# At the border to the second layer: four first row sums by VectorE, all x tiles turned before the products, source terms kept by ScalarE

## The reference, cut to what matters

```
# layer 1 (a graph attention; x is what the first layer left)
Wh = x @ W
e_src = Wh @ a[:d_out]
e_dst = Wh @ a[d_out:]
e = leaky_relu(e_src[:, None] + e_dst[None, :], 0.2)
mask = (adj > 0) | eye(N)
alpha = softmax(where(mask, e, -9e15), axis=1)
x = layernorm(x + alpha @ Wh)
# layers 2 and 3 (graph convolutions) use these sums of the same rows of adj:
rowsum = adj.sum(axis=1)
```

## Time and profile before

| | us |
|---|---|
| median of 3 runs | 3029.25 (3028.38 to 3029.67) |
| the profiled execution | 3032.35 |
| its span, from the first to the last instruction | 3030.6 |
| TensorE busy | 2951.2 (97%) |
| VectorE busy | 2098.9 (69%) |
| ScalarE busy | 1885.9 (62%) |
| GpSimd busy | 769.0 (25%) |

### The profile page before, as it was taken

How to read it: one execution, slowest core, us unless ns; L and a number is a source line. 1 busy time by engine, 2 the same in 40 slices (tenths; PEclk the granted TensorE clock), 3 DMA queues, 4 the chain that set the end, 5 groups by cost and what they waited for, 6 DMA issues and landing times.

```text
span 3030.6 us, 45417 instructions
## 1 busy us (share of the span) xinstructions
PE 2951.2 (97%) x16612; PEld 2181.2 (72%) x16612; DVE 2098.9 (69%) x3607; ACT 1885.9 (62%) x2705; POOL 769.0 (25%) x454
## 2 busy tenths in 40 slices
PE   8999999999999999999998899999999999999998
PEld 5777777777777777777776555555558888788886
DVE  6777777777777877787757977777535555565454
ACT  3677777777777777777775677777653333433332
POOL 2123321233212332133301455545501101000000
PEclk9999999999999999999999999999999999999999
DMA  6556676566755667566636333433179988989882
GB/s 186 158 170 198 198 211 180 170 197 196 216 162 180 199 188 227 156 184 205 189 101 257 124 125 130 148 126 125 32 183 214 214 200 201 221 209 217 199 200 58
DMA packets 412525, 534.42 MB, mean 176 GB/s; under 512 B 39440, under 2 KB 341776, under 8 KB 395920
## 3 DMA queue, kind: packets, MB, share of 16 engines
q1 hardware_dynamic: 387264, 445.00, 52.8%
q10 hardware_dynamic: 18144, 66.07, 7.1%
q0 software_dynamic: 6896, 20.45, 2.3%
HBM read 443.29 MB, written 88.08 MB: 175 GB/s over the span
## 4 chain that ended last, share of the span: by engine, by line
PE 80%; DVE 9%; issue 5%; DMA 3%; ACT 2%; POOL 1%; SPq 1%; DVEq 0%; POOLq 0%; ACTq 0%
PE at_o L609 12%; PE gl_four L1479 12%; PE at_turn L583 9%; PE at_turn L596 7%; PE gl_quad L1532 7%; PE gl_quad L1533 7%; PE gl_quad L1534 7%; PE at_score L583 4%; PE at_score L596 4%; PE gl_quad L1462 3%; DVE at_probs L869 2%; DVE at_bias L820 2%; PE gl_four L1505 2%; PE at_mixed L618 2%; DMA adjT<-at_probs 1%
## 5 line engine op out<-in xcount | busy, mean ns | idle before, releaser
L720 ACT ACTIVATE at_probs<-at_probs,at_minus_max 128x1024 f32<-128x1024 f32 x512 | 581.6, 1139 | 9.7 <-DVE at_minus_max L874 8.8
L869 DVE CUSTOM_DVE_ANT_0 at_probs<-at_turn,at_bias 128x1024 f32<-128x1024 f32 x336 | 407.3, 1212 | 170.2 <-PE at_turn L583 164.0
L506 POOL TENSOR_SCALAR at_masked<-at_bias 128x512 bf16<-128x512 f32 x180 | 378.2, 2116 | 537.7 <-DMA at_bias<-in_adj 405.4
L729 ACT ACTIVATE at_pT<-at_turn 128x1024 f32<-128x1024 f32 x342 | 346.0, 1024 | 235.4 <-PE at_turn L596 235.3
L609 PE MATMUL at_o<-at_pT,at_values 128*64 128x256 f32 x4096 | 470.3, 382 | 0.0
L1479 PE MATMUL gl_four<-gl_early,gl_first_wh 128*128 128x512 f32 x1024 | 462.3, 594 | 4.6 <-ACT gl_early L1604 4.6
L1629 ACT ACTIVATE gl_split<-gl_units 128x1024 fp32r<-128x1024 f32 x256 | 263.8, 1055 | 278.6 <-PE gl_quad L1534 278.6
L1532 PE MATMUL gl_quad<-gl_split,gl_rows_hi 128*128 128x512 f32 x1024 | 402.3, 393 | 5.0 <-DVE gl_split L1817 5.0
L609 PEld LDWEIGHTS at_o<-at_pT,at_values 128*64 128x64 f32 x4096 | 282.4, 137 | 172.8 <-issue 43.2
L583 PE MATMUL at_turn<-at_kT,at_q 128*128 128x512 f32 x1344 | 396.0, 416 | 10.3 <-DVE at_maxima L869 10.3
L1533 PE MATMUL gl_quad<-gl_split,gl_rows_hi 128*128 128x512 f32 x1024 | 398.5, 389 | 0.0
(11 more groups left out here) (135 smaller groups left out, 3871.0 us busy)
## 6 DMA issues: line engine op xcount, KB each, us to landing
gl_units<-adjT SPq DMA_DIRECT2D x512, 256.0 KB, 7.8
at_bias<-in_adj SPq DMA_DIRECT2D x128, 512.0 KB, 6.5
at_probs<-in_adj SPq DMA_DIRECT2D x256, 256.0 KB, 3.7
adjT<-at_probs SPq DMA_DIRECT2D x1024, 64.0 KB, 3.0
gl_first_weights<-in_adj SPq DMA_DIRECT2D x32, 2048.0 KB, 8.2
at_values<-v_heads ACTq DMA_DIRECT2D x126, 512.0 KB, 4.4
gl_early<-x SPq DMA_DIRECT2D x160, 128.0 KB, 2.6
x<-gl_early POOLq DMA_DIRECT2D x64, 128.0 KB, 2.8
```

Of the source, the lines that this page charges most:

```text
L506: pool.tensor_scalar(masked[:, g % MASKS, :], part, 0.0, MASKED / SCALE, ALU.is_equal, ALU.mult)\
L720: act.activation(part, part, ACT.Exp, bias=minus_max[:, k, t:t + 1], scale=1.0, accum_out=sums[:, k, t, pp:pp + 1]).then_inc(prob_ready, 1)
L729: act.activation(pT[:, j % PT_SLOTS, :], place[:], ACT.Copy).then_inc(pT_ready, 1)
L869: dve.tensor_tensor_reduce(out=ring[:, place_in_ring(u, pp), t, :], in0=place[:], in1=bias[:, t, at], scale=SCALE, scalar=LOWEST, op0=ALU. ...
```

## The change

Eight things change.

1. VectorE adds and masks only items 0 to 3 in the attention's last beats (`DVE_ROWS = 4`, two beats and not six).
2. ScalarE adds items 4 to 19: one behind each kept x unit 0 to 6 (`ROWS_BY_X`), the others behind kept Wh units (`ROWS_BY_WH`).
3. By the same rule as before, GpSimd now masks the odd items above 4 but 15: items 5, 7, 9 and 11 come to it beside 13. VectorE masks 4, 6, 8 and 10 later.
4. `v_xT` has 8 places, one for each unit, and takes the last two quarters of the second chunk's `weights`.
5. TensorE first turns x and makes the target terms for units 0 to 6 in a row, then makes Wh of units 0 and 1, turns the last unit, and makes the other Wh.
6. ScalarE keeps the source terms, in halves of two right behind each half of Wh (`keep_src`, scale -1); the next `make_wh` waits half by half.
7. Maxima, masks and logits on VectorE are put in a new order.
8. On SyncE, x tiles 16 to 29 come before adj quarter 2, x tiles 30 and 31 before the third quarter of the second chunk; that quarter waits for the Wh of four units and the fourth for all eight.

```diff
-    XT_RING = 4
-    DVE_ROWS = 12
+    DVE_ROWS = 4
-        v_xT = view(weights, HALF_BIG + 3 * CT * QC, XT_RING, DH * CN)
+        v_xT = view(weights, HALF_BIG + 2 * CT * QC, CHUNKS, DH * CN)
-        EARLY_ROWS = {0: (12, 13), 1: (14, 15), 2: (16,), 3: (17,), 4: (18,), 5: (19,)}
-        ROWS_IN_BEAT = {24: (0, 1), 25: (2, 3), 26: (4, 5), 27: (6, 7), 28: (8, 9), 29: (10, 11)}
+        ROWS_IN_BEAT = {24: (0, 1), 25: (2, 3)}
+        ROWS_BY_X = {u: (4 + u,) for u in range(CHUNKS - 1)}
+        ROWS_BY_WH = {0: (11, 12), 1: (13,), 2: (14, 15), 3: (16,), 4: (17,), 7: (18, 19)}
+        LAST_MASKS = (12, 14, 15)
+        WH_BEFORE_LAST = 2
...
-            if at == 23:
-                load_first_adj(sync, 2)
             if at == 25:
                 sync.wait_ge(shared.turned, shared.turned_but_one)
                 load_x(sync, 16, 30, 1)
+                load_first_adj(sync, 2)
                 load_first_adj(sync, 3)
...
-            sync.wait_ge(shared.turned, shared.beats)
+            load_x(sync, 30, 32, 2)
+            sync.wait_ge(wh_made, NT // 2)
             load_adj(1, 2)
-            load_x(sync, 30, 32, 2)
             sync.wait_ge(wh_made, NT)
             load_adj(1, 3)
...
             def make_wh(u):
-                wait(pe, wh_read, u)
...
                 for t in range(CT):
+                    if t % 2 == 0:
+                        wait(pe, wh_read, 2 * u - 1 + t // 2)
...
-            turn_x(pe, 1)
-            make_dst(0)
-            turn_x(pe, 2)
-            make_dst(1)
-            make_dst(2)
+            for u in range(CHUNKS - 1):
+                if u + 1 < CHUNKS - 1:
+                    turn_x(pe, u + 1)
+                make_dst(u)
             for u in range(CHUNKS):
-                if u + 3 < CHUNKS:
-                    turn_x(pe, u + 3)
+                if u == WH_BEFORE_LAST:
+                    turn_x(pe, CHUNKS - 1)
+                    make_dst(CHUNKS - 1)
                 if u == CHUNKS - 2:
                     turn_w()
                 make_wh(u)
-                if u + 3 < CHUNKS:
-                    make_dst(u + 3)
...
+            def keep_src(u, part):
+                m = CT * u + 2 * part
+                act.activation(minus_src[:, m:m + 2], quad[:, 2 * part:2 * part + 2, D:D + 1].rearrange("p a b -> p (a b)"),
+                               ACT.Copy, scale=-1.0).then_inc(wh_read, 1)
...
-                if c == 0:
-                    dve.wait_ge(wh_read, 1)
+                dve.wait_ge(wh_read, 2 * (c + 1))
...
-            def keep_src(u):
-                dve.wait_ge(wh_kept, 2 * (u + 1))
-                dve.tensor_scalar(minus_src[:, CT * u:CT * (u + 1)], quad[:, :, D:D + 1].rearrange("p a b -> p (a b)"),
-                                  -1.0, None, ALU.mult).then_inc(wh_read, 1)
...
+            masks(10)
+            for e in (10, 11):
+                read_max(e)
+            for e in LAST_MASKS:
+                masks(e)
+            for half in range(2):
+                if half == 1:
+                    keep_dst(CHUNKS - 1)
+                for e in LAST_MAXIMA:
+                    read_half_max(e, half)
+            make_shift(0)
+            for e in range(6):
+                logits(e)
+            keep_w()
+            for e in (16, 18):
+                masks(e)
+            for e in range(6, 10):
+                logits(e)
```

More of the change, by code:

```diff
@@ L1410, in make_dst @@
                 for half in range(DH):
-                    last = pe.matmul(upper[2 + u % 2], wa_wide[:, half, :], v_xT[:, u % XT_RING, half * CN:(half + 1) * CN],
+                    last = pe.matmul(upper[2 + u % 2], wa_wide[:, half, :], v_xT[:, u, half * CN:(half + 1) * CN],
                                      start=half == 0, stop=half == DH - 1)
@@ L1456, in turn_pair @@
                 if g < 2:
-                    pe.wait_ge(wh_read, CHUNKS)
+                    pe.wait_ge(wh_read, 2 * CHUNKS)
                 wait(pe, pT_ready, g - 1)
@@ L1632, in keep_xT @@
                 act.wait_ge(v_turned, u + 1)
-                wait(act, wh_made, CT * (u - XT_RING + 1))
-                act.activation(v_xT[:, u % XT_RING, :], four[:, 0:DH, :].rearrange("p a b -> p (a b)"), ACT.Copy)\
+                act.activation(v_xT[:, u, :], four[:, 0:DH, :].rearrange("p a b -> p (a b)"), ACT.Copy)\
                    .then_inc(v_ready, 1)
```

51 lines of the change are left out of this document (20 added, 31 removed).

## The result

| | before | after |
|---|---|---|
| median of 4 runs, us | 3029.46 (3028.38 to 3033.88) | 3012.37 (3006.57 to 3013.94) |
| profiled execution, us | 3032.35 | 3011.64 |
| its span, us | 3030.6 | 3009.5 |

The ratio is 0.9937, with a 95% interval of 0.992 to 0.9955: 14 to 24 us faster, where differences from 6 us on can be told from none. When the changed kernel was run again, its median was 3010.81 and the ratio 0.9936 (0.9923 to 0.9948). The forecast was 3010, the range 3004 to 3018.

A forecast was written before the change was run, and what follows sets the result against it. TensorE, busy 97% of the span, was taken as the bound, losing time idle or at half clock. First L1479 at 1669.3 against 1688.49 gives 19.2 us: 3032.35 - 19.2 = 3013.1 profiled, 3010 median; range 3004 to 3018.

The forecast's parts named there:

- Row sums hold back L908: Attention's end on VectorE: unneeded row sums delay the final L908; without them it comes at 1614.2, not 1626.15, 12 us sooner.
- The row of seven units: TensorE's turns and target terms for units 0 to 6: 2.59 us per unit, no long waits, ending at 1631.7.
- The small W just in time: Weight load the first products need: lands at 1631.6, as the row of turned units ends at 1631.7.
- x tiles 30 and 31: Input of the last turn: issued in the deferred 2 MB quarter's place, landing at 1638.7 instead of 1643.7, just in time.
- rival of late tiles: x tiles 30 and 31 still land at 1643.7: 4 us less gain, 15, or 3014; chance 0.10.
- The bubble: TensorE before the last target terms: 2.1 us idle, as the last turn's copy stands behind other ScalarE work.
- The end: Last products to loop: products end 1665.2 including 0.4 for halves, first turned pair 1666.1, first L1479 1669.3 after 3.2.
- The shift: VectorE chain from item 15's row sum at 1649.9 to the shift at 1656.8; 0.3 us short of deciding the end.
- The masks: GpSimd's four new masks beside VectorE operations: 0.85 us each, 3.4 in all, mostly where VectorE waits anyway.
- rival of whole-mask exclusion: VectorE waits a whole GpSimd mask, 4.12 us and not 0.85: some 8 us less gain, 11, or 3018; chance 0.06.
- An unmoved tail: Rival at the attention's end: final L908 stays at 1626 for another reason; 9.3 us less gain, or 3019; chance 0.04.
- TensorE at half clock: Rival in the border: clock falls at the first small gap and stays, 48 us of work take 96, 3058; chance 0.03.

The follow-up runs named there:

- Experiment 2: Changed kernel with VectorE again adding and masking items 0 to 11, adj quarter 2 ahead of x tiles; border 65.97 us, median 3022.24, ratio 0.9974 to the kernel before.
- experiment 7: Changed kernel with adj quarter 2 issued ahead of x tiles 16 to 29, as before; border 57.02 us, single execution 3012.31.
- experiment 1: Kernel before with only the source terms moved to ScalarE, kept in halves; border 65.83 us, median 3020.07, ratio 0.9974 to the kernel before.
- Experiment 6: Changed kernel with the small W issued behind the second quarter of the second chunk, not ahead; border 62.43 us, one execution 3017.49.
- Experiment 9: Changed kernel with row sums, last unit's target terms, small W, exponentials and first pairs' waits rearranged to close gaps; border 54.56 us, median 3009.47, ratio 0.993 to before.
- experiment 8: Changed kernel with the masks of items 5, 7, 9 and 11 on VectorE, not GpSimd; border 57.02 us, single execution 3011.24.
- 3: Changed kernel with TensorE's old order, products between the turned units; border 66.12 us, median 3020.62, ratio 0.9971 to the kernel before.
- 4: Changed kernel with source terms given back to VectorE, once per unit; border 64.10 us, median 3019.71, ratio 0.9968 to the kernel before.
- Experiment 5: Kernel before with idle matmuls added in TensorE's two long waits; border 72.47 us, one execution 3025.38 against 3031.49.

## Why the prediction was right, point by point

*Row sums hold back L908.* Right. The final L908 was predicted at 1614.2 and came at 1612.36, which is 1614.2 on the prediction's clock. Experiment 2 brings the wait back by undoing nothing but the row sums, their masks and the place of one transfer, which experiment 7 shows to cost nothing. One thing the prediction passed over: "nothing but row sums stands between" is not all, for these sums themselves waited 3.56 us for adj quarter 1 (experiment 1). Taking them away took both away, so the step holds.

*The row of seven units.* Right: pitch 2.59, predicted end 1631.7, measured 1630.12, or 1631.9 on the prediction's clock. ScalarE was idle for 0.53 us ahead of most copies and never late.

*The small W just in time.* Right, as a knife's edge: 0.40 us of wait in one profile of the change, none in the other. It landed at 1630.4, that is 1632.2 against a predicted 1631.6. With it the products began 0.6 late (1630.52, or 1632.3, against 1631.7), and 0.5 of lateness was left at the end of the sum. Experiment 6 shows the edge from its other side.

*x tiles 30 and 31.* Predicted to land at 1638.7, just in time. SyncE issued them at 1623.86, and this is their row (the counterpart of the earlier trace rows):

```profile
gl_first_wh<-x SPq DMA_DIRECT2D x1, 256.0 KB, 12.9
```

They landed at 1636.8, or 1638.6, and the last turn did not wait. The rival of late tiles did not come true; at the measured turn (1637.55) the slack was 0.8 us. They were issued 1.3 us later than predicted (1625.7 on its clock, not 1624.4) and landed on time all the same.

*The bubble.* 1.82 us against 2.1. The cause is as told, but in two parts: the turn ends at 1638.58, item 13's sum holds the copy until 1639.33, and the copy itself takes 1.02. Experiment 9 closes it with two edits at once, the sum moved and a product put between turn and target terms; moving the sum alone would leave some 1.1 of it (an estimate from these rows).

*The end.* The 0.4 us for waits on halves was 0.18, but the step after it was read wrongly. The prediction had the first turned pair wait for ScalarE, held up by the fourth exponential, 0.9 us behind the last product (1665.2 to 1666.1). In fact ScalarE was through with the exponentials at 1663.2, copied one half and then itself waited 0.46 us for the last product. That product ended at 1664.28, and the 0.84 us ahead of the first L1461 are a plain handover: copy of its half, source terms, turn. That 0.84 came where 0.9 was predicted is luck. The last product ended 0.9 later than predicted (1666.1 on its clock), and the step from L1461 to L1478 was 2.90 and not 3.2, which gave 0.3 of it back.

*The shift.* Said to be 0.3 us short of deciding; it came at 1656.27, or 1658.1 and not 1656.8, and ScalarE's first exponential waited 0.43 us. Item 15's sum came 0.5 later, and the small operations between the last maximum and the shift take 1.2 us, not 0.7. The 0.5 more is in one of them, L1760, which took 0.66 us beside GpSimd's mask of item 17:

```profile
1654.78 3.67 POOL L1174 TENSOR_SCALAR gl_first_weights<-gl_first_weights 128x1024 f32<-128x1024 f32 x1 [9.70 <-ACT gl_first_weights L1585]
```

Before, no mask ran at this place, and the same step took 0.16. The step was mis-sized, at a price of 0.2 us at most: the 0.18 ahead of the last product waits for a copy that stands behind the first two exponentials. In experiment 9 it is what limits the version.

*The masks.* VectorE's operations beside a GpSimd mask took 1.51 instead of 0.69 (twice), 1.45, and 1.44 instead of 1.21: 0.2 to 0.8 us each, 2.6 in all for the masks of items 5 to 13, where 3.4 were set down for four; in the second profile of the change the most was 0.84 (2.05 for 1.21). They cost nothing, being ahead of a wait of 4.59. The wait of 0.81 for item 11's mask came in the same place. The rival of whole-mask exclusion is refuted: no such operation waited for the 3.7 to 4.6 us of a mask, and without four of the masks (experiment 8) VectorE reached its wait at the same time, where over 3 us sooner was the rival's sign. The rule of the Trainium skill (page "SBUF — State Buffer", section "SBUF: two separate sides"), that the two exclude each other for a whole instruction, does not describe these rows; the measurement decides.

*An unmoved tail, and TensorE at half clock.* Neither: L908 moved, and the clock was 1.00 through the border although the row has gaps of 0.34 to 1.82 us.

*The loop keeps the gain.* Right, 1341.48 against 1342.11. The median of 3012.4 instead of 3010 is 0.5 us of the sum and otherwise scatter: the second set of runs gave 3010.8. The border itself came 18.66 us shorter in one profile and 19.20 in the other, against 19.2; so close a hit is luck in part, since terms of 0.3 to 0.9 us were off both ways, and since the 76.32 of before would have been 74.4 with adj quarter 1 landing as in experiment 2.

## What to carry to other kernels

When an engine waits in one place for one thing, ask what it would wait for next if that came early: here the vector engine's late sum hid a weight load that lands 6 us later, and removing either cause alone gained 1 us at most, both together over 9. Fill the time until a transfer lands with work that doesn't need it, and measure a change of a few microseconds between two marks in the profile rather than in the total, whose scatter is larger. If that stretch scatters too, look for the transfer whose landing moves it, and count from there. A small copy that another engine waits for belongs on the engine that already reads the same buffer, right behind that read.

## What the runs showed of the hardware

An idle stretch of TensorE costs clock beyond itself, and several kernels here show how much. The matmuls behind a wait of 7.74 us (before) took 2.5 us longer than at full clock, behind 5.42 us 3.1, behind 7.64 us (experiment 1) 2.8, behind 7.15 us (2) 1.65, behind 9.05 us (3) 1.8, behind 3.49 us (6) 1.7. Behind 1.82, 1.49 and 1.56 us (after, 4, 9) nothing was lost: the granted clock stayed at 1.00. The loss does not grow with the wait; it was 1.6 to 3.1 us at each of these six. Experiment 5 showed it to be clock, since idle matmuls without any use removed it at two of them, and also that not all of it need be the kernel's loss: of the 2.5 us at the first only 0.7 came back.
